# Mean squares of queries and keys as two products of rounded parts with ones, small vectors inside the constants' transfer, and newly planned orders on five engines

## The reference, cut to what matters

```
def _rms(x):
    return x * jax.lax.rsqrt(jnp.mean(x * x, axis=-1, keepdims=True) + EPS)
qkv = _rms(x) @ w_qkv.T
q, k, v = jnp.split(qkv, 3, axis=-1)
q = _rms(q)
k = _rms(k)
w = jnp.exp(k)
y = jax.nn.sigmoid(q) * (cumsum(w * v) / (cumsum(w) + 1e-06))
uv = y @ w_swiglu.T
```

## Time and profile before

| what | value |
|---|---|
| median of 3 runs (lowest, highest) | 506.53 us (505.81, 506.99) |
| span of the profiled execution | 506.1 us |
| PE busy | 489.5 us, 97% of the span |
| DVE, ACT, POOL busy | 342.6 (68%), 297.2 (59%), 275.6 (54%) us |
| granted clock of PE, mean | 0.997 |
| transfers | 55.35 MB, 109 GB/s over the span |

### The profile page before, as it was taken

How to read it: one execution, slowest core, us unless ns; L and a number is a source line. 1 busy time by engine, 2 the same in 40 slices (tenths; PEclk the granted TensorE clock), 3 DMA queues, 4 the chain that set the end, 5 groups by cost and what they waited for, 6 DMA issues and landing times.

```text
span 506.1 us, 7336 instructions
## 1 busy us (share of the span) xinstructions
PE 489.5 (97%) x2418; PEld 374.1 (74%) x2418; DVE 342.6 (68%) x732; ACT 297.2 (59%) x590; POOL 275.6 (54%) x253
## 2 busy tenths in 40 slices
PE   7999999989999999999999999999998999999997
PEld 5455557767887678879888888877766767677785
DVE  6999999898989999558989996224232322322347
ACT  5897898978899678589456343354331342323220
POOL 0163758749474566473634466847765665555500
PEclk9999999899999999999999999999999999999999
DMA  8900003004532011044105675722244222222177
GB/s 305 331 2 0 0 2 124 2 0 159 175 126 87 2 42 43 1 133 155 59 2 180 204 233 184 253 84 77 84 135 144 75 82 76 73 73 80 67 283 236
DMA packets 20245, 55.35 MB, mean 109 GB/s; under 512 B 3361, under 2 KB 6097, under 8 KB 20209
## 3 DMA queue, kind: packets, MB, share of 16 engines
q1 hardware_dynamic: 15696, 42.56, 24.7%
q0 software_dynamic: 4512, 12.33, 7.8%
HBM read 37.18 MB, written 17.74 MB: 109 GB/s over the span
## 4 chain that ended last, share of the span: by engine, by line
PE 71%; ACT 7%; POOL 6%; DMA 5%; issue 5%; DVE 4%; another core or an unknown queue 1%; SPq 0%; DVEq 0%; ACTq 0%
PE bank L317 50%; PE bank L510 9%; DMA y_rows<-m_y,dest 5%; PE bank L411 3%; POOL y_rows L1508 2%; POOL xg L1496 2%; PE bank L499 1%; PE bank L543 1%; PE bank L384 1%; ACT L643 1%; PE bank L570 1%; DVE m_y L1356 1%; PE bank L458 1%; ACT fd L729 1%; PE bank L400 1%
## 5 line engine op out<-in xcount | busy, mean ns | idle before, releaser
L1508 POOL DMA_INDIRECT y_rows<-m_y,dest x47 | 47.5, 1010 | 38.9 <-DVE m_y L1356 30.4
L1356 DVE TENSOR_SCALAR m_y<-bank,gslot 128x256 f32<-128x256 f32 x47 | 22.3, 483 | 61.1 <-DMA y_rows<-m_y,dest 36.6
L317 PE MATMUL bank<-mw,m_xt 128*128 x188 | 61.5, 463 | 0.8 <-DVE hs L1233 0.6
L1496 POOL DMA_INDIRECT xg<-xn_rows,tab x47 | 45.6, 971 | 20.2 <-issue 10.5
L317 PE MATMUL bank<-yhr,wsg_h 128*128 128x512 f32 x128 | 52.8, 412 | 0.0
L317 PE MATMUL bank<-hyr,wsg_h 128*128 128x512 f32 x128 | 50.0, 391 | 0.0
L317 PE MATMUL bank<-yhr,wsg_l 128*128 128x512 f32 x128 | 49.9, 390 | 0.0
L317 PE MATMUL bank<-mw,m_ht 88*128 x188 | 46.2, 381 | 3.1 <-DVE m_y L1356 2.0
L317 PEld LDWEIGHTS bank<-mw,m_xt 128*128 128x128 f32 x188 | 33.6, 189 | 17.8 <-issue 4.5
L1437 POOL TENSOR_TENSOR tk<-tk 128x512 f32<-128x512 f32 x16 | 21.0, 1315 | 38.0 <-ACT tk L787 37.9
L317 PEld LDWEIGHTS bank<-mw,m_ht 88*128 88x128 f32 x188 | 33.8, 190 | 8.7 <-issue 4.0
(11 more groups left out here) (272 smaller groups left out, 1393.5 us busy)
## 6 DMA issues: line engine op xcount, KB each, us to landing
mw<-in_gu SPq DMA_DIRECT2D x16, 352.0 KB
ga<-y_rows SPq DMA_DIRECT2D x8, 512.0 KB, 6.7
mw<-in_dn SPq DMA_DIRECT2D x16, 176.0 KB
wsg_w<-in_wsg SPq DMA_DIRECT2D x4, 512.0 KB, 4.2
spilled_x<-fa SPq DMA_DIRECT2D x4, 512.0 KB, 2.8
hx<-spilled_x SPq DMA_DIRECT2D x4, 512.0 KB, 4.6
xn_rows<-fg SPq DMA_DIRECT2D x4, 512.0 KB, 4.1
spilled_y<-fa SPq DMA_DIRECT2D x4, 512.0 KB, 3.0
```

Of the source, the lines that this page charges most:

```text
L317: mm = e.matmul(o, a, b, start=n == 0, stop=n == len(terms) - 1)
L1356: e.tensor_scalar(m_y[j % 3][:, :], ps("jd", j)[:, 0:D], gslot[:, j:j + 1], None, ALU.mult).then_inc(s["jy"], 1)
L1496: e.indirect_dma_start(out=xg[j % GATHERED][:, :], out_offset=None, in_=xn_d, in_offset=bass.IndirectOffsetOnAxis(ap=tab[:, j:j + 1], axis ...
L1508: e.indirect_dma_start(out=y_d, out_offset=bass.IndirectOffsetOnAxis(ap=dest[:, j:j + 1], axis=0), in_=m_y[j % 3][:, :], in_offset=None).t ...
```

## The change

- `meanq` and `meank` become two products in the fast format. The sum of squares is rounded (`qkround`, ACT, new), the rest is made (`qklow`, POOL, new), and each is multiplied by a matrix of ones. The ones are `w_one`, now made for 128 partitions instead of 96; `oproj` uses 96 of them as before. The division by 256 moves into the logarithm's scale.
- `w_vec` goes: its ten columns are inside `w_cst`, in the first part of its transfer. One transfer and its issue fall away.
- In `dact` the table load stands ahead of the waits. One `logexp()` is added on ACT ahead of `normal2(1, 2)`.
- `kphi` of blocks 2 and 3 waits for `wvsum` too, `xback`, `yback` and `unpark` wait for `dg` as well as `du`, and `breathe` waits for the table of tiles.
- All five lists are in new orders, and PE's steps have new banks. PE has the same 487 calls.

```
             def meanq(b, n):
                 o = take(("mq", b), n, s["rq"], 2 * b + 1)
-                q.wait_ge(d["rest"], loaded["rest"])
-                q.wait_ge(s["sqf"], b + 1)
-                e.matmul(o[:, :], mean, FC[b % 2][:, 0, :], start=True, stop=True).then_inc(s["mq"], 1)
+                q.wait_ge(s["sqf"], 2 * b + 2)
+                products(o[:, :], [(w_one[:, :], FCr[b % 2][:, j, :]) for j in (1, 0)]).then_inc(s["mq"], 1)
...
-                e.activation(w_one[:, :], mean[0:96, :], ACT.Copy, scale=float(D)).then_inc(s["bor"], 1)
+                e.activation(w_one[:, :], mean, ACT.Copy, scale=float(D)).then_inc(s["bor"], 1)
...
+            def qkround(b, k):
+                q.wait_ge(s["skf" if k else "sqf"], 2 * b + 1)
+                e.activation(FCr[b % 2][:, 1, :], FC[b % 2][:, 0, :], ACT.Copy).then_inc(s["bor"], 1)
...
-                e.activation(r, ps(key, b)[:, :], ACT.Ln, bias=con(C_RMS)).then_inc(t, 1)
+                e.activation(r, ps(key, b)[:, :], ACT.Ln, bias=con(C_RMS), scale=1.0 / D).then_inc(t, 1)
...
             def dact(b, k):
                 c, m = CHUNKS * b + k, chunk_of(k)[4]
+                if DIRECT[b]:
+                    table("silu_and_others")
+                else:
+                    table("exp_and_others", "silu_and_others")
                 if c > 1:
                     q.wait_ge(s["dw"], c - 1)
                 q.wait_ge(s["dg"], c + 1)
...
+            def qklow(b, k):
+                q.wait_ge(s["bor"], 3 + 2 * b + k + 1)
+                e.tensor_tensor(FCr[b % 2][:, 0, :], FC[b % 2][:, 0, :], FCr[b % 2][:, 1, :].bitcast(F32), ALU.subtract).then_inc(s["skf" if k else "sqf"], 1)
...
-            fetch(0); fetcht(); consts(); load('vec', w_vec, vec); load('wc', w_wc, wc); fetch(1); efetch(); load('qkv1', qkv1_w, wqkv1)
+            fetch(0); fetcht(); consts(); load('wc', w_wc, wc); fetch(1); efetch(); load('qkv0', w_qkv0, wqkv0); stagein(4); stagein(5)
```

More of the change, by code:

```diff
@@ L582, in tensor @@
[L582 to L605, removed]
@@ new lines, in tensor @@
+            vproj(1, 0, 5); vproj(1, 1, 4); emturn(1, 1, 2); eproject(0, 1); eproject(1, 0); logits(1, 3, 3); express(1, 0, 2); turnr(0, 0, 5); turnr(0, 1, 4)
+            turn2(0, 0, 1); qproj(1, 0, 0); turn2(0, 1, 5); qproj(1, 1, 1); qproj2(0, 0, 3); qproj2(0, 1, 4); express(1, 1); emturn(1, 2, 5); emturn(1, 3, 0)
+            kproj2(0, 0, 1); express(1, 2); express(1, 3); meanq(0, 5); kproj2(0, 1, 0); dgate(0, 0, 5); dgate(0, 1, 3); gates(0, 4); ffn(1, 0, 2); ffn(1, 1, 5)
+            ffn(1, 2, 3); ffn(1, 3, 4); meank(0, 2); dup(0, 0, 5); oproj(1, 0, 3); oproj(1, 1, 4); vproj2(0, 0, 2); vproj2(0, 1, 5); dup(0, 1, 1); dgate(0, 2, 0)
@@ new lines, in tensor @@
+            turnr(1, 0, 3); turnr(1, 1, 4); ddown(0, 0, 6, 7); qproj2(1, 0, 2); qproj2(1, 1, 5); kproj2(1, 0, 3); kproj2(1, 1, 4); meanq(1, 1); vproj2(1, 0, 0)
+            dup(0, 2, 1); turn2(1, 0, 2); turn2(1, 1, 5); vproj2(1, 1, 1); emturn(2, 0, 2); emturn(2, 1, 5); express(2, 0, 2); meank(1, 5); ddown(0, 1, 6, 7)
+            express(2, 1); gates(1, 5); dup(0, 3, 3); dup(0, 4, 4); ddown(0, 2, 6, 7); dgate(0, 3, 0); dgate(0, 4, 1); dgate(0, 5, 5); dgate(0, 6, 0)
+            dgate(0, 7, 1); dgate(0, 8, 3); dup(0, 5, 4); ddown(0, 3, 6, 7); ddown(0, 4, 6, 7); dup(0, 6, 5); emturn(2, 2, 4); dup(0, 7, 0); emturn(2, 3, 5)
@@ new lines, in tensor @@
+            ddown(0, 10, 6, 7); turn2(2, 0, 2); turn2(2, 1, 4); dgate(1, 1, 0); gates(2, 2); turnr(2, 1, 4); dup(1, 0, 5); emturn(3, 2, 0); emturn(3, 3, 3)
+            express(3, 1); express(3, 2); express(3, 3); qproj2(2, 0, 4); qproj2(2, 1, 5); ffn(3, 0, 0); ffn(3, 1, 3); dup(1, 1, 2); dup(1, 2, 1); ffn(3, 2, 0)
+            ffn(3, 3, 2); dgate(1, 2, 3); meanq(2, 0); ddown(1, 0, 6, 7); kproj2(2, 0, 2); kproj2(2, 1, 0); oproj(3, 0, 4); oproj(3, 1, 5); vproj2(2, 0, 3)
+            meank(2, 1); vproj2(2, 1, 4); dgate(1, 3, 5); dgate(1, 4, 1); ddown(1, 1, 6, 7); ddown(1, 2, 6, 7); turn2(3, 0, 2); turn2(3, 1, 0); dup(1, 3, 3)
@@ new lines, in tensor @@
+            dup(1, 4, 4); dup(1, 5, 5); turnr(3, 0, 1); turnr(3, 1, 2); gates(3, 0); dgate(1, 5, 3); dgate(1, 6, 4); ddown(1, 3, 6, 7); ddown(1, 4, 6, 7)
+            route1(1); dup(1, 6, 0); dgate(1, 7, 2); qproj2(3, 0, 3); qproj2(3, 1, 5); dgate(1, 8, 4); ddown(1, 5, 6, 7); ddown(1, 6, 6, 7); meanq(3, 0)
+            kproj2(3, 0, 1); kproj2(3, 1, 0); dup(1, 7, 2); dup(1, 8, 3); dgate(1, 9, 5); dup(1, 9, 4); dup(1, 10, 2); meank(3, 3); ddown(1, 7, 6, 7)
+            ddown(1, 8, 6, 7); dgate(1, 10, 3); routed(0, 1); route2(0); routed(1); vproj2(3, 0, 5); vproj2(3, 1, 4); dgate(2, 0, 3); dgate(2, 1, 2); routed(2)
@@ L634, in tensor @@
+            ddown(3, 5, 6, 7); ddown(3, 6, 6, 7); dup(3, 9, 3); dup(3, 10, 5); ddown(3, 7, 6, 7); dgate(3, 10, 2); ddown(3, 8, 6, 7); ddown(3, 9, 6, 7)
             ddown(3, 10, 6, 7)
```

329 lines of the change are left out of this document (163 added, 166 removed).

## The result

| kernel | median us | ratio to the kernel before, 95% interval |
|---|---|---|
| before, beside it | 506.76 | |
| changed | 532.83 | 1.0515 (1.0485 to 1.0545) |

A forecast was written before the change was run, and what follows sets the result against it. PE, 97% busy, was taken as bound where DVE and ACT do not set the pace, after some 200 us. -3.2 + 1.0 + 1.35 - 0.3 - 0.6 = -1.75 from 506.1, plus 0.4: 504.8, said 504.7; range 500.3 to 508.8.

The forecast's parts named there:

- I put 0, with 3 us either way: Among the experts, 350 to 480 us: moving dgate, dup and ddown out costs nothing, PE staying longer than POOL.
- the added waits on `dg` and for the table of tiles: On SP's and POOL's lists: put at nothing, things long done when asked for; named as what could hold them.
- The prediction's own sign: Among the experts: the forecast is wrong if PE's loss there, 5.9 us before, changes by over 3 us.
- The cover for scatters: Among the experts: five dgate or dup and four ddown, 12.7 us, covered scatter waits; their leaving was put at 0.
- POOL becomes the experts' bound: Rival, among the experts: POOL needs over 119 us and PE waits 2 to 4 us; 507 to 509 us, chance 0.11.
- The means: Eight query and key means: cheaper products save 3.2 us of PE's work; three late means cost 1.0 us.
- nothing is left: Rival: blocks 0 and 1 give nothing, the others' 1.6 us is eaten by a new wait; 506 to 507, chance 0.16.
- The new chains hold PE: Rival, at the means: subtractions meet DVE's two-operand work, chains take 3.1 us instead of 2.1; 509 us, chance 0.11.
- the locking out of POOL by DVE: At the new subtractions: DVE work with two SBUF inputs may cost each mean some 1.0 us more.
- The order ahead of `qproj2(1, 0)`: Ahead of this PE step, waiting for DVE's rlow: less work as cover, so PE waits 1.35 us longer.
- The start: Kernel start: without w_vec ACT begins about a microsecond earlier; gain 0.3 us, between 0 and 1.
- The table load: In dact, at 331.83 us: the load starts in the wait; gain 0.6 us, between 0 and 0.8.

The follow-up runs named there:

- experiment 1: Changed kernel with experts(14) moved ahead of experts(15) and yback(3) in SP's list: 519.54 us, ratio 1.0268.
- experiment 3: Kernel before with yback(3) moved ahead of experts(14) and experts(15) in SP's list: 514.23 us, ratio 1.0156.
- experiments 4 and 5: Changed kernel with its 16 expert loads where the kernel before has them, 519.37 us; then onehot(5), refine(3), routed(4) to (6) moved too, 511.47 us.
- experiment 8: Changed kernel with expert loads, onehot(5), refine(3), routed(4), rback(3) reordered, unparks one dup and dgate later, routed(5), (6) behind dup(2, 5): 505.51 us, ratio 0.9982.
- experiment 9: Kernel before with the new means alone, six of the eight one or two places later on PE: 522.09 us, ratio 1.028.

## Why the prediction was wrong

**The step that failed** is the one that put the orders of the lists at nothing: "I put 0, with 3 us either way" for the experts, and no term at all for what stands ahead of the first `xup`. The place that was named, "the added waits on `dg` and for the table of tiles", was not the one: SP stood for some 0.1 us ahead of `yback(3)`. What held PE was the place of a load, experts(14) behind experts(15) and behind the 512 KB of `yback(3)`. The prediction's own sign came true: PE's loss among the experts changed by over 3 us, from 5.9 to 10.2. By the scatters the price of the load's place is about 5.4 us; moving it gave 13.3 (experiment 1), and the like fault cost 7 in the kernel before (experiment 3).

**Two more lists** were not priced at all: `onehot(5)` beside POOL's 1024 columns, and `routed(4)` and `refine(3)` placed later. Together they held 8 us (experiments 4 and 5). Of DVE I had said that it is nearly full in the first 200 us; in the changed kernel it is busy without a gap from 284 to 300 us as well.

**The cover for scatters** was named ("they were cover for the wait on scatters") and rated at 0. The wait grew from 2.0 to 4.34 us and took the clock with it. Its price is the 5.3 us of experiment 8, which took the unparks away and brought no cover back. Whether the cover that left, or POOL's order of the scatters, made it longer than before is not shown. The rival "POOL becomes the experts' bound" did not come: in experiment 8 POOL is busy for 83.55 of 130 us there and PE loses 1.4.

**The low clock** was in no term. The earlier trace rows has 0.96 from 60 to 100 us, and I did not ask what it stood for. In the changed kernel each of the waits of over 3 us had two or more windows of 4 us with a lower clock, in which PE had work; that adds 2.6 to 2.9 us to each, so that a wait cost up to nearly twice its length. It does not account for the earlier trace rows, though: there the clock is 0.89 and 0.68 from 92 to 100 us while PE is busy for 3.87 and 4.00 of 4 us, and no run shows why.

**The means.** Right in their parts: the chain is 2.15 us longer (fold done at 118.09, product at 120.24; 2.1 was said), and a pair of products saves 0.4 us where PE sets the pace, in blocks 2 and 3 (1.45 us of the 1.6 foreseen, from one trace each). Wrong in blocks 0 and 1, where I had -1.6 + 1.0 = -0.6: they lose about as much as the others save. That is the rival "nothing is left" for this term. "The new chains hold PE" came true in the old orders, and not by the way that was given: of the eight subtractions seven took 1.27 to 1.29 us and one 1.90, so the locking out of POOL by DVE cost next to nothing there (in experiment 9 the longest took 1.58 us). It was POOL's wait for ACT's rounding, 0.74 us at best and 3.36 at worst.

The lock itself, by the Trainium skill (SBUF — State Buffer, "Who interferes with whom"), shuts a VectorE instruction with two SBUF inputs and a GpSimd instruction that reads SBUF out against each other. The trace agrees, at a place where I had not looked: 2.90 us for 0.68 at 294.00.

**The order ahead of `qproj2(1, 0)`**: 2.40 us of wait, from 1.11 + 1.35 = 2.46. Right. **The start**: wrong as a gain. `w_cst` was in at 6.15 us and ACT began at 6.17 instead of 5.73. In the twelve traces of this study with the vectors in `cst` ACT began between 4.53 and 6.17 us, in the four without between 5.51 and 5.90, so one execution does not tell a term of 0.3 us. **The table load**: the wait is gone; alone it is too small to be measured.

**What stays open.** ACT stood 5.74 us from 424.36 and 5.43 from 456.51 in the changed kernel, each time for something that the profile calls another core or an unknown queue. PE lost 1.14 us at 430.82 and 2.7 at 462 to 464, and the low clock behind it. They are not in the profile of experiment 1, whose lists are the same but for the one load, and this is where nearly 10 of its 15.1 us between the spans arise. So more than a third of the whole loss has no cause shown: it went away when the load was moved, by a path that no run was made for.

## What to carry to other kernels

Where written-out lists change, compare on each queue what stands ahead of a transfer that somebody will need: what the calls ahead of it wait for, and how many bytes they put in front of it. In a kernel like this one, price a wait of PE of 3 us or more with the low clock behind it, up to nearly twice. When one edit gives back more than the wait that it removes, follow one kind of step through both traces, to see where the rest came from. And an operation added to a lightly used engine costs by what is queued behind it, when it must wait for a third engine.
